# A selective-scan and attention kernel on one Trainium2 core: the four gate products at a unit's start each stand one scan later

## The reference, cut to what matters

```python
def step(hst, ins):
    dt_t, B_t, C_t, x_t = ins
    dA = jnp.exp(dt_t[:, :, None] * A)
    hst = hst * dA + (dt_t * x_t)[:, :, None] * B_t[:, None, :]
    y_t = jnp.einsum('bds,bs->bd', hst, C_t)
    return (hst, y_t)
...
y = jnp.swapaxes(ys, 0, 1) + xs * Dskip
return y * jax.nn.silu(z) @ out_w
```

## Time and profile before

| what | value |
|---|---|
| time, median of 3 runs | 3474.05 us (3472.1 to 3475.24) |
| the profiled execution | 3473.82 us, span 3472.0 us |
| PE busy | 3320.5 us, 96% of the span |
| DVE busy | 2981.9 us, 86% |
| ACT busy | 2902.2 us, 84% |
| POOL busy | 2305.9 us, 66% |
| chain of work that ended last | PE 73%, ACT 12%, DVE 7%, POOL 3%, issue 3%, DMA 1% |

### The profile page before, as it was taken

One profiled execution on the slowest core, in us unless ns is written; L12 is line 12 of the kernel. 1 busy time (PEld: TensorE's weight loads), 2 busy tenths in 40 slices (PEclk: granted clock), 3 DMA queues, 4 the chain that ended last, 5 costly groups with the idle time before them and its releaser, 6 DMA issues.

```text
span 3472.0 us, 59905 instructions
## 1 busy us (share of the span) xinstructions
PE 3320.5 (96%) x22946; PEld 2561.0 (74%) x22946; DVE 2981.9 (86%) x2916; ACT 2902.2 (84%) x4709; POOL 2305.9 (66%) x1087
## 2 busy tenths in 40 slices
PE   8999999999999999999999999999899989999999
PEld 5888988898898888988988898898786432222344
DVE  4988999999999999999999999999996688888231
ACT  6999999999999999999999999999994437777620
POOL 1878998898898889988988988899685000000000
PEclk8999999999999999999999999999999989999999
DMA  3223222222222222222222222222211241220000
GB/s 114 74 71 79 80 68 71 64 69 69 69 85 69 68 65 74 69 71 63 76 69 70 63 69 68 65 69 69 78 61 34 55 110 19 37 31 7 0 7 19
DMA packets 193185, 214.21 MB, mean 62 GB/s; under 512 B 75617, under 2 KB 144993, under 8 KB 192641
## 3 DMA queue, kind: packets, MB, share of 16 engines
q1 hardware_dynamic: 192898, 210.36, 21.2%
HBM read 192.19 MB, written 18.06 MB: 61 GB/s over the span
## 4 chain that ended last, share of the span: by engine, by line
PE 73%; ACT 12%; DVE 7%; POOL 3%; issue 3%; DMA 1%; SPq 0%; DVEq 0%; ACTq 0%; POOLq 0%
PE psum L1534 19%; PE psum L1309 18%; PE psum L1528 14%; PE psum L1525 11%; ACT arena L967 5%; ACT arena L950 4%; DVE arena L1215 3%; PE psum L1621 3%; PE psum L1610 3%; POOL arena L725 3%; PE psum L1585 2%; DVE row_max L1262 2%; PE psum L1554 1%; POOL arena L709 1%; DVE skip_w L1288 1%
## 5 line engine op out<-in xcount | busy, mean ns | idle before, releaser
L725 POOL TENSOR_TENSOR arena<-arena 128x1024 f32<-128x1024 f32 x1024 | 2236.6, 2193 | 377.4 <-DVE arena L1215 355.2
L1215 DVE TENSOR_TENSOR_SCAN arena<-arena,psum 128x512 f32<-128x512 f32 x2048 | 2377.4, 1230 | 118.6 <-PE psum L1528 76.2
L967 ACT ACTIVATE arena<-arena,a_neg 128x512 f32<-128x512 f32 x2048 | 1421.0, 713 | 48.7 <-PE psum L1528 48.2
L1534 PE MATMUL psum<-ident,arena 128*128 128x128 f32 x8192 | 1241.7, 275 | 8.0 <-POOL arena L725 7.9
L950 ACT ACTIVATE arena<-arena,bT 128x512 f32<-128x512 f32 x1536 | 1095.8, 714 | 0.0
L1528 PE MATMUL psum<-ident,arena 128*128 128x128 f32 x6144 | 1016.3, 275 | 0.0
L1534 PEld LDWEIGHTS psum<-ident,arena 128*128 128x128 f32 x8192 | 968.4, 142 | 14.1 <-POOL arena L725 12.9
L1525 PE MATMUL psum<-arena 128*128 128x128 f32 x4096 | 838.7, 287 | 75.2 <-DVE arena L1215 62.3
L1525 PEld LDWEIGHTS psum<-arena 128*128 128x128 f32 x4096 | 652.1, 192 | 307.7 <-issue 177.1
L1528 PEld LDWEIGHTS psum<-ident,arena 128*128 128x128 f32 x6144 | 749.9, 143 | 0.0
L1309 PE MATMUL psum<-arena 128*128 128x512 f32 x1472 | 705.3, 601 | 11.6 <-issue 5.1
(11 more groups left out here) (120 smaller groups left out, 1097.0 us busy)
## 6 DMA issues: line engine op xcount, KB each, us to landing
arena<-bc_dram SPq DMA_DIRECT2D x256, 512.0 KB, 3.7
arena<-diag_dram SPq DMA_DIRECT2D x224, 128.0 KB, 2.1
arena<-qk_dram SPq DMA_DIRECT2D x96, 128.0 KB
diag_dram<-arena SPq DMA_DIRECT2D x32, 256.0 KB, 4.5
qk_dram<-arena SPq DMA_DIRECT2D x12, 512.0 KB, 4.9
arena<-in_x SPq DMA_DIRECT2D x4, 512.0 KB, 10.5
arena<-in_up_w SPq DMA_DIRECT2D x1, 2048.0 KB, 11.2
out_xT<-arena SPq DMA_DIRECT2D x8, 256.0 KB, 2.3
```

The source lines that it names most:

```text
L725: pool.tensor_tensor(out[:, :, way], h_now[:, :, way], c_row, ALU.mult)\
L967: act.activation(decay[:, w % AHEAD, f], dt_[:, u % 2, f], ACT.Exp, scale=a_neg[:, d, f, st:st + 1])\
L1215: dve.tensor_tensor_scan(hs[:, w % RING, f, rows][:, way], decay[:, w % AHEAD, f, way], psum[:, 4 + n % U_BANKS, way], end_state(w - DS, f ...
L1534: return pe.matmul(psum[:, c, f * P:(f + 1) * P], hs[:, w % RING, f, at:at + P], ident[:, :], is_transpose=True, start=False, stop=w % DS ...
```

## The change: where the gate products stand

In the first steps of the units 1 to 7, gate product c stood behind scan (1, c). Now it stands behind the scan after that one: products 0, 1 and 2 behind scans (1, 1), (1, 2) and (1, 3), product 3 behind scan (2, 0). Nothing is added or taken away: 28 gate products in all are moved. The four products of the last unit, behind its last scan, stay.

```diff
-                        if u and st == 1:
-                            gate_y(u - 1, f)
+                        if u and st == 1 and f:
+                            gate_y(u - 1, f - 1)
+                        if u and st == 2 and f == 0:
+                            gate_y(u - 1, NI - 1)
```

## The result

The changed kernel takes 3457.61 us (median of 6 runs, 3455.81 to 3459.1), the kernel before 3472.58 us (median of 6 in the same comparison, 3470.84 to 3475.24). The ratio is 0.9956 with a 95% interval of 0.9943 to 0.9969: 15 us less, between 11 and 20. The profiled execution took 3455.81 us, its span is 3454.0 us.

The account below looks back on a forecast made before the run. Waits between DVE and PE at the starts of units 1 to 7 were taken as the bound. 8.0 + 1.2 + 4.85 - 0.1 = 13.95, say 14.0 us, from 3474.05: forecast 3460.0, range 3457.5 to 3467.5 for 8 in 10.

Parts of the forecast that it names:

- Can PE follow?: Unit starts: PE can fill banks 1.17 us earlier, with 0.26 us slack at scan (3, 0); only unit 3 loses 0.1.
- What bounds the start: Starts of units 1 to 7: DVE waits for PE's last sum, then PE 2.06 us for scan (1, 1) queued behind.
- Kept later: Stretches after the starts, such as steps 13 to 32 at 97.8 us, keep their lengths, so the gain stays.
- Terms 1 and 2: Starts: scan (1, 1) under DVE's wait, 8.0 us; PE's lateness in units 2, 4, 6, 1.2 us.
- the margin of the later gate products: Start, columns 1 onward: gate products come every 1.8 us, PE needs 2.0; margin 0.2 us, growing with each column.
- Term 3: Starts of units 3, 4, 6: three clock falls go as PE's idle time shrinks, 4.85 us.
- The rival by which they stay: Clock falls are a matter of phase, as many occur there or elsewhere: 3464.9 us; chance 0.28.
- the forecast of no gain: Starts: the wait changes its name, ACT or POOL sets the pace; 3474 us, or 3469.6 if odd units alone; chance 0.11.
- the slower rival: Starts: PE's pause splits in two, the clock falls behind each; 3482.8 us with both in all seven units; chance 0.04.

Follow-up runs that it names:

- odd_only: Gate products moved one scan later in units 1, 3, 5, 7 alone, against the kernel before: 3465.52 us, ratio 0.9979.
- even_only: Gate products moved one scan later in units 2, 4, 6 alone, against the kernel before: 3464.49 us, ratio 0.9977.
- skip_first: Changed kernel with first_state's wait for POOL's products moved behind the four skip matmuls of column 0: 3458.17 us, ratio 0.9956.
- short_dtx: Changed kernel with POOL's four extra dt*x products per unit done for 32 of 512 columns: 3453.24 us in its one run.
- two_later: Changed kernel with each gate product one scan later still, two later than before: 3460.57 us, ratio 0.9965.
- block_of_gates: Changed kernel with all four gate products in a row behind scan (1, 1): 3464.13 us, ratio 0.9975.
- pe_filler: Kernel before with 16 unread 128x128 matmuls on PE behind the last sum of each unit: 3475.57 us, ratio 1.0009.
- after: First profile of the changed kernel: the profiled execution took 3455.81 us.
- after_b: Second profile of the changed kernel, nothing altered: 3459.34 us.

## Where the prediction held, and the steps that failed

The mechanism held. Two steps of the sum failed, in opposite directions. "Can PE follow?" took 0.1 us off for PE's lateness in the odd units, and it was 1.2 us. And the sum, with its range, had no term for the time outside the seven starts: it went from a base of 3474.05 and put the low end 2.5 us below the forecast, while that outside time differs by 5.0 us between the two profiled executions. That the time still came within 2.4 us of the forecast is in part luck: the first error made the forecast gain too large, the second the forecast time too long.

**What bounds the start: right.** DVE waited for PE's sum with a scan behind it that PE needed next. The gate products' seven waits fell to 1.5 us (about 0.3 each were forecast, 2.1), the 2 us ahead of `turn_u(2, 0)` are gone from all seven starts, and `odd_only` and `even_only` show the gain unit by unit.

**Kept later: right.** Steps 13 to 32 of unit 1, from 462.92 in the kernel after, took 97.83 us (97.82 before). Of the six stretches between the starts, five have the same length in both profiles to 0.04 us, and that in unit 2 is 0.5 us shorter after. A gain at a start is handed on whole.

**Terms 1 and 2: right in the even units, too large in the odd ones.** Against the starts of before without a fall, the even ones lose 17.60 - 16.08 = 1.52 us each, 4.6 in all; 3.4 + 1.2 = 4.6 were forecast. The odd ones lose 1.18, 0.56, 0.91 and 0.83, together 3.5 us, where 4 x 1.17 = 4.7 less 0.1 was forecast. The step that failed is "Can PE follow?", with its slack of 0.26 us at scan (3, 0). PE and DVE in unit 3 of the kernel after:

```profile
1039.72 1.13 PE L1556 MATMUL psum<-skip_w,arena 128*128 128x128 f32 x8 [1.31 <-POOL arena L725]
1040.69 0.60 PE L1536 MATMUL psum<-ident,arena 128*128 128x128 f32 x4
...
1046.99 0.49 PE L1530 MATMUL psum<-ident,arena 128*128 128x128 f32 x3
```

```profile
1047.62 8.38 DVE L1215 TENSOR_TENSOR_SCAN arena<-arena,psum 128x512 f32<-128x512 f32 x7 [0.43 <-PE psum L1530]
```

The bank is full at 1046.99 + 0.49 = 1047.48 and the scan that waited for it starts at 1047.62. So by the trace's times 0.14 of the supposed slack is the way from PE to DVE. The other 0.12 gave nothing either: what an odd start gains is what column 0 gains, up to one scan. In unit 3 column 0 stands 1039.72 - 1035.05 = 4.67 us behind scan (1, 0), in unit 5 it is 4.33. In unit 5 of the kernel before it was 1683.84 - 1678.59 = 5.25:

```profile
1683.84 0.94 PE L1554 MATMUL psum<-skip_w,arena 128*128 128x128 f32 x7
```

That is 0.58 and 0.92 us earlier, against 0.56 and 0.91 measured. The row of unit 3 that I took, 1047.10, was itself 0.1 us late, since the slow stretch had begun at 1046.84. The units 5 and 7, for which the full 1.17 us were reckoned, had not been read at all. `skip_first` gave unit 3 its 0.6 us back.

A smaller reading of that step was also too generous. In the kernel before, columns 0 and 1 of `first_state` start 414.67 - 412.79 = 1.88 us apart, not 2.0, so the margin of the later gate products was 0.1 us and not 0.2:

```profile
414.67 1.06 PE L1554 MATMUL psum<-skip_w,arena 128*128 128x128 f32 x8
```

It held all the same: PE's waits after have no row for a gate product.

**Term 3: right.** The falls at the starts went, all three, 4.85 us as forecast. The rival by which they stay fell with 63 starts without one. The rule of the Trainium skill that I set against the term ("TensorE: Matmul & The Clock Gate", Part 1: The HAM clock gate), a free-running window and no specific count, agrees with the three profiles of the kernel before: 3, 4 and 3 of seven starts were struck, in two profiles the same units and in one others. The inference that I drew from it, that the falls would stay as many or turn up elsewhere, is what the runs refute. With 10 falls in three profiles the kernel before pays 5.4 us on average rather than 4.85. Nor do all falls go: those at other places, late in the units and in unit 0, come with or without the change.

**The other rivals.** ACT didn't hold unit 1: its start is the one odd start with the full gain, 1.18 us. It stays 0.13 us or more above the other odd starts in `short_dtx` and `skip_first`, with ACT busy all through it; what holds that rest is not shown. POOL did hold column 0 in the odd units, but for 3.9 us in four of them and never beyond 4.67 us behind scan (1, 0), where the forecast of no gain needed 5.38. The second stop of PE, which the slower rival needed for its extra falls, exists (0.54 to 1.31 us) and brought none.

**The sum and the range.** 14.0 us were forecast, 13.0 came at the starts of the profiled pair and 15.0 in the medians, whose interval is 11 to 20. Over three profiles of before and two of after the starts hold 13.5 on average. The medians give 3457.61 for a forecast of 3460.0. The forecast gain would give 3472.58 - 14.0 = 3458.6 from the base that six runs show, and the time lies 1.0 us below that. So most of the distance is the base: the three runs before had their median at 3474.05, 1.5 us above that of six. The low end, 3457.5, was too tight: the median lies 0.1 us above it and three of six runs below. I had set it from a spread of 3.1 us and had not asked what moves a run by that much. The part ahead of unit 1's start, which the change doesn't touch, does it by up to 3.5 us. An estimate from these 3.5 us, taken off the 3458.6, would have put the low end at 3455.

## What to carry to other kernels

When an engine waits for the last result of one stage, look at what is queued behind the wait and whether its next partner needs it: one instruction of the next stage moved ahead of the wait can end two waits at once. Of the places tried, the best is where the wait is almost used up; past it (`two_later`), or with everything pushed back at once (`block_of_gates`), the other engine starts to wait for what was moved. Read the slack of the follower from a row in which it really was waited for, since the way of a signal looks like slack elsewhere.

## What the runs showed of the hardware that I had not expected

- At the unit starts, PE's pauses of 2.0 us were followed by a granted clock of 0.50 for 3.4 us in 12 of 28 cases, at 1.6 us each; starts whose longest pause is 1.3 us or less had none in 63. Elsewhere in the same kernel a fall did come with two stops of 1.27 and 0.94 us close together. Eight matmuls that nobody reads, put into the pause, saved 4.5 us of 3473 (ratio 0.9987, 0.9978 to 0.9997) with no other change.
- What a fall costs depends on where it comes: 1.6 us at a start, 0.04 us late in unit 1, in a stretch of 301 us.
- A plain fp32 matmul of 128x128 on a 128x128 operand took 3.57 / 16 = 0.22 us here and stands in the trace as two records, where the transposes on line 1534 (1535 in `pe_filler`, four from 407.86 to 408.30) take 0.11 us and one record each.
- Two profiles of one program (`after`, `after_b`) differ by 2.4 us in a stretch of 335 us, with 0.95 and 0.96 as its mean clock. A pair of profiles is no measure of a change of a few us; the stretch that the change touches is.
